# Matmuls of zeros between the first maximum passes and between the last scores of a cross-attention and expert kernel

## The chip, the core and the metric

The kernel runs on one core of a Trainium2 chip. A core has TensorE (matmuls, writing to PSUM, PE in the profile), VectorE (DVE), ScalarE (ACT), GpSimd (POOL) and DMA queues that SyncE (SP) and others fill. The metric is the device time of one execution in microseconds; the lower the better. A time is given as the median of several runs, and one further execution was recorded by the hardware profiler.

## What is computed

Eight samples x of 256 channels by 512 positions get a cross attention with 16 heads of 16 channels each (queries from the layer-normed x, keys and values from a context), and then a mixture of eight experts, two per row, with a shared expert. Cut to the attention:

```python
q = einsum('oc,bct->bot', Wq, layernorm(x)) + bq      # k and v from ctx, with Wk, Wv
q = q.reshape(B, H, K, T)                             # H = 16 heads, K = 16, T = 512
scores = einsum('bhkt,bhks->bhts', q, k) * SCALE
p = softmax(scores, axis=-1)
out = einsum('bhts,bhks->bhkt', p, v).reshape(B, H * K, T)
x = x + einsum('oc,bct->bot', Wo, out) + bo
x = x + ffn(layernorm(x))    # rmsnorm, router, top 2 of 8 experts, and a shared expert
```

## The kernel before

The attention is cut into 16 halves (`HALVES`): a half is eight heads of one sample. Each half has 32 units (`UNITS`): a unit is one head and one quarter (128) of the 512 positions.

For a softmax without overflow the kernel first needs the maximum of each row of scores. So it computes scores twice. A **maximum pass** (`max_pass`, line 560, tile `smax_ps`, three banks) multiplies queries by keys with the queries' positions on the partitions; VectorE reduces each bank to a column of `negmax` (line 665, semaphore `max_done`). When a half's 32 units are done, `turn_max` (line 574) transposes the maxima, VectorE splits them into two parts (lines 672 and 674), and the SP queue carries them to DRAM and back into two extra rows of the query stack (lines 337 and 345, semaphore `rows_loaded`). The **scores** proper (`scores`, line 586, tile `st_ps`, three banks) then come out with the maximum subtracted, and ScalarE takes their exponential into `probs` (line 490, `exp_done`). After each group of four units a step `pv` (line 599, tile `pv_ps`) multiplies the probabilities by the values; after four such steps ScalarE copies the sums out (line 481), and they travel over DRAM to be divided. Maximum passes and scores use only 48 or 50 of the array's 128 rows, and two of them, of different row halves, run side by side.

The tensor engine's order is written out by hand. First four opening matmuls of zeros (line 510), then the projections of the halves 0 and 1 (`project_qk`, line 533, and `project_v`, line 544). Then the prologue: all 32 maximum passes of half 0, with the projections of half 2 in between; `turn_max(0)`; and the first 24 (`LEAD`) passes of half 1. Then the main loop over slots s = 0 to 15: for each pair of units two scores of half s, two maximum passes 24 units ahead, and at fixed u a `pv` step, a projection of half s + 3, the turn of the maxima, or (in odd slots, `OUT_UNITS`) a step of the output projection (`project_out`, line 232). In slot 14 the passes end at u = 6; from u = 8 there, and in all of slot 15, no maximum passes are left, and no projections but four steps of the output projection late in slot 15.

A score for unit i waits for the exponential of unit i - 3, since there are three banks; a maximum pass for unit i waits for the reduction of unit i - 3. VectorE, between the maxima of half 0 and those of half 1, computes row statistics of the last samples (line 246). Behind the main loop comes the stage of the shared expert and routing, and then 39 expert blocks (lines 1045 to 1086). `zeros` is a tile of 128 by 512 zeros in fp32 that VectorE sets at the start.

Of the kernel before, what the change touches and what calls it, by code (L numbers as in the profile page):

```python
# [13 lines left out]
P = 128  # L14
# [3 lines left out]
HALVES = 2 * B  # L18
# [3 lines left out]
GH = 4  # L22
UNITS = HH * TT
STEPS = UNITS // GH
LEAD = 24
# [4 lines left out]
TILES = 2  # L30
# [16 lines left out]
def xattn_ffn_kernel(nc, x, ctxt, wqkv_t, wo_t, bias_cols, rms_w, router_t, gate_up, down,  # L47
# [18 lines left out]
    with ExitStack() as outer:  # L66
        def sem(name):
            return outer.enter_context(nc.semaphore(name))

        def sb(name, shape, dt=F32, stack=outer):  # L70
            return stack.enter_context(nc.sbuf_tensor(name, shape, dt))
# [3 lines left out]
        zeros = sb("zeros", [P, D])  # L75
# [28 lines left out]
        def aps(name, shape, dt=F32):  # L104
            return attn_ctx.enter_context(nc.psum_tensor(name, shape, dt))
# [16 lines left out]
        pv_ps = aps("pv_ps", [P, T])  # L122
# [23 lines left out]
        max_done = sem("max_done")  # L146
# [38 lines left out]
        def out_batch(s):  # L185

            return (s - 3) // 2 if s % 2 == 1 and s >= 3 else None

        def smax_bank(i):
            return smax_ps[:, i % MAXBUF, :]  # L190
# [34 lines left out]
        def project_out(pe, b, o, kt, bank):  # L225
            if kt == 0 and o == 0:
                pe.wait_ge(attn_ready, ATTN_START + 2 * (b + 1))
                pe.wait_ge(vt_copied, min(2 * b + 7, HALVES))
                pe.wait_ge(nm_parts_ready, min(2 * b + 5, HALVES))
            if kt == 0 and (b > 0 or o > 0):  # L230
                pe.wait_ge(x1_ready, X1_START + 2 * b + o)
            mm = nc.tensor.matmul(bank, w_o[:, kt, o * P:(o + 1) * P], attn[:, b % 2, kt, :],  # L232
                                  start=(kt == 0), stop=(kt == CT - 1))
            if kt == CT - 1:
                mm.then_inc(y_ready, 1)
# [63 lines left out]
        with nc.Block() as block:  # L299
# [207 lines left out]
            def _(pe):  # L507
# [5 lines left out]
                for o in range(CT):  # L513
                    for kt in range(CT):
                        mm = nc.tensor.matmul(pv_ps[:, o:o + 1], w_o[:, kt, o * P:(o + 1) * P], bv_col[:, kt:kt + 1],
                                              start=(kt == 0), stop=(kt == CT - 1))
                mm.then_inc(bo_ready, 1)

                def project_qk(n, i, kt):
                    if kt == 0 and i == 0:  # L520
                        pe.wait_ge(c_loaded[(n // 2) % 2], 16 * (n // 4 + 1))
                        if n >= FIRST:
                            pe.wait_ge(vt_copied, n)
                            pe.wait_ge(nm_parts_ready, n - 2)
                        if out_batch(n - 4) is not None:
                            pe.wait_ge(x1_ready, X1_START + CT * (out_batch(n - 4) + 1))
                        if 1 <= n < 3:
                            pe.wait_ge(vt_copied, n)
                    elif kt == 0:
                        pe.wait_ge(qk32_ready, 2 * n + 1)  # L530
                        pe.wait_ge(xn_ready, n // 2 + 1)
                    src = c_sb[:, (n // 2) % 2, :, :] if i == 0 else xn
                    mm = nc.tensor.matmul(proj_ps[:, :], w_t[:, i, kt, (n % 2) * P:(n % 2) * P + P],  # L533
                                          src[:, kt, :], start=(kt == 0), stop=(kt == CT - 1))
                    if kt == CT - 1:
                        mm.then_inc(qk_ready, 1)

                def project_v(n, st):
                    if st == 0:
                        pe.wait_ge(qk32_ready, 2 * n + 2)  # L540
                        if n >= FIRST:
                            pe.wait_ge(nm_parts_ready, n - 1)
                    for kt in range(CT):
                        mm = nc.tensor.matmul(proj_ps[:, st * P:(st + 1) * P],  # L544
                                              c_sb[:, (n // 2) % 2, kt, st * P:(st + 1) * P],
                                              w_t[:, 2, kt, (n % 2) * P:(n % 2) * P + P],
                                              start=(kt == 0), stop=(kt == CT - 1))
                    if st == TT - 1:
                        mm.then_inc(v_ready, 1)

                def max_pass(n, u):
                    buf = n % NBUF
                    if u == 0:
                        pe.wait_ge(stack_loaded[buf], 16 * 2 * 2 * TILES * (n // NBUF + 1))
                    i = UNITS * n + u
                    if i >= MAXBUF:
                        pe.wait_ge(max_done, i - MAXBUF + 1)
                    tile, pair, tt = u % TILES, u // TILES // TT, u // TILES % TT
                    low = HALFP * tile
                    nc.tensor.matmul(smax_bank(i), q_stack[buf][low:low + SROWS, pair, tt * P:(tt + 1) * P],  # L560
                                     k_stack[buf][low:low + SROWS, pair, :], start=True, stop=True,
                                     tile_position=(low, 0)).then_inc(s_ready, 1)

                def turn_max(n):
                    if n == 0:
                        pe.wait_ge(vt_copied, FIRST)
                    else:
                        pe.wait_ge(qk32_ready, 2 * min(n + 3, HALVES))
                        pe.wait_ge(vt_copied, min(n + 2, HALVES))
                        pe.wait_ge(nm_parts_ready, n)  # L570
                    if n > 0 and out_batch(n - 2) is not None:
                        pe.wait_ge(x1_ready, X1_START + CT * (out_batch(n - 2) + 1))
                    pe.wait_ge(max_done, UNITS * (n + 1))
                    nc.tensor.transpose(proj_ps[0:UNITS, 0:P], negmax[:, n % 2, :], ident[:, :]).then_inc(nm_turned, 1)

                def scores(s, u):
                    g, st, j = u // (GH * TT), u // GH % TT, u % GH
                    buf = s % NBUF
                    if u == 0:
                        pe.wait_ge(rows_loaded[buf], 16 * TILES * (s // NBUF + 1))  # L580
                        pe.wait_ge(ones_loaded, 16 * TILES * NBUF)
                    i = UNITS * s + u
                    if i >= STBUF:
                        pe.wait_ge(exp_done, i - STBUF + 1)
                    low, pair, end = HALFP * (j % TILES), 2 * g + j // TILES, HALFP * (j % TILES) + SROWS + PARTS
                    nc.tensor.matmul(score_bank(i), k_stack[buf][low:end, pair, st * P:(st + 1) * P],  # L586
                                     q_stack[buf][low:end, pair, :], start=True, stop=True,
                                     tile_position=(low, 0)).then_inc(st_ready, 1)
# [16 lines left out]
                for n in range(2):  # L605
# [3 lines left out]
                    for st in range(TT):  # L609
                        project_v(n, st)  # L610
                pe.wait_ge(ident_ready, 2)
                for u in range(UNITS):
                    max_pass(0, u)
                    if u in (0, 2, 8, 10):
                        project_qk(2, u // 8, u % 8 // 2)
                    if 16 <= u < 16 + TT:
                        project_v(2, u - 16)
                turn_max(0)
                for u in range(LEAD):
                    max_pass(1, u)  # L620

                for s in range(HALVES):
                    proj = s + 3 < HALVES
                    for u in range(0, UNITS, TILES):
                        scores(s, u)
                        scores(s, u + 1)
                        n = s + 1 + (u + LEAD) // UNITS
                        if n < HALVES:
                            max_pass(n, (u + LEAD) % UNITS)
                            max_pass(n, (u + LEAD) % UNITS + 1)  # L630
                        if u % GH == 0 and STEPS * s + u // GH >= 1:
                            pv(STEPS * s + u // GH - 1)
                        if proj and u in (0, 2, 6, 8):
                            project_qk(s + 3, u // 6, u % 6 // 2)
                        if proj and 14 <= u < 14 + 2 * TT:
                            project_v(s + 3, (u - 14) // 2)
                        if u == 12 and s + 1 < HALVES:
                            turn_max(s + 1)
                        if out_batch(s) is not None and u in OUT_UNITS:
                            project_out(pe, out_batch(s), OUT_UNITS.index(u) // CT, OUT_UNITS.index(u) % CT, proj_ps[:, :])  # L640
                pv(STEPS * HALVES - 1)
# [650 lines left out]
```

## Time and profile before

| | before |
|---|---|
| median of 3 runs | 988.53 us (981.55 to 991.89) |
| the profiled execution | 987.59 us |
| its span, first to last instruction | 985.7 us |
| mean granted TensorE clock | 0.903 |
| TensorE busy | 885.4 us, 90% |
| VectorE busy | 463.3 us, 47% |
| ScalarE busy | 408.1 us, 41% |

A row of the profile's timeline gives the start in us from the span's start, the duration in us, the engine, the line of the kernel, the operation, and its output and input tiles by name; behind it the idle time before it and who ended that. Several instructions of one kind in a row are merged, x2 and so on; each then lasts a little beyond the start of the next row, since matmuls are pipelined. A matmul of fp32 operands stands as two instructions; a score or a maximum pass (fp32r) as one. PE is TensorE's matmul, PEld its weight load. The granted clock is given as a share of full speed (2.4 GHz).

### The profile page before, as it was taken

Reading aid. Unit: us, or ns where it says so; the run is one execution under the profiler, and the core shown is the slowest. Engines: PE = TensorE matmul, PEld = TensorE weight load, DVE = VectorE, ACT = ScalarE, POOL = GpSimd, SP = SyncE. Lnnn points to the kernel's source line nnn. Section 1 sums busy time; section 2 is a strip of 40 time slices with the busy share of each in tenths; the row PEclk is TensorE's granted clock in tenths of the full one; section 3 lists DMA queues with packets and bytes.
Section 4 is the critical chain, followed back from the end, with each engine's and each line's share of the span. In section 5 each row is a group of like instructions: output and inputs, shape, how many; then the busy total and the mean of one; then the engine's idle time right before and its main releaser. Section 6 shows DMA issues by size and latency. Waiting matters only on the chain. (4 is left out here: it accounts for less than half of the span.)

```text
span 985.7 us, 10816 instructions
## 1 busy us (share of the span) xinstructions
PE 885.4 (90%) x3616; PEld 376.5 (38%) x3616; DVE 463.3 (47%) x894; ACT 408.1 (41%) x753; POOL 253.6 (26%) x239
## 2 busy tenths in 40 slices
PE   7679999898998989999998998899399999999992
PEld 3233333333333333333332225654144444444441
DVE  3577777676776765777786006451121111111110
ACT  1103676655666565666667542320002222222320
POOL 3100221413214131231110000317312444444431
PEclk8755999999999997999997557989699999999997
DMA  6772455546645565255521104941132455545552
GB/s 218 191 174 94 114 135 132 132 90 151 143 101 128 94 153 127 64 130 132 130 51 27 24 22 155 393 171 44 45 111 60 86 89 96 93 87 88 92 88 32
DMA packets 47877, 110.56 MB, mean 112 GB/s; under 512 B 12704, under 2 KB 13728, under 8 KB 43520
## 3 DMA queue, kind: packets, MB, share of 16 engines
q1 hardware_dynamic: 35376, 80.26, 31.7%
q0 software_dynamic: 12416, 29.48, 14.6%
q8 instruction: 31, 0.51, 0.2%
q14 instruction: 22, 0.18, 0.1%
q10 hardware_dynamic: 32, 0.13, 0.0%
HBM read 68.48 MB, written 41.23 MB: 111 GB/s over the span
## 5 line engine op out<-in xcount | busy, mean ns | idle before, releaser
L665 DVE TENSOR_REDUCE negmax<-smax_ps 128x1 f32<-128x512 f32 x512 | 325.5, 683 | 131.1 <-PE smax_ps L560 130.0
L490 ACT ACTIVATE probs<-st_ps 128x512 f32<-128x512 f32 x512 | 273.7, 603 | 155.1 <-PE st_ps L586 154.9
L586 PE MATMUL st_ps<-q_stack,k_stack 50*128 50x512 f32 x512 | 163.9, 522 | 20.5 <-ACT probs L490 20.5
L560 PE MATMUL smax_ps<-k_stack,q_stack 48*128 48x512 f32 x512 | 144.0, 456 | 13.9 <-DVE negmax L665 7.3
L599 PE MATMUL pv_ps<-probs,v_t 128*32 128x512 f32 x1024 | 148.9, 656 | 3.6 <-ACT probs L490 1.7
L1086 PE MATMUL big_ps<-w_gu,attn 128*128 x312 | 140.4, 593 | 0.8 <-ACT attn L934 0.8
L586 PEld LDWEIGHTS st_ps<-q_stack,k_stack 50*128 50x128 f32 x512 | 63.0, 197 | 178.0 <-ACT probs L490 116.4
L898 POOL DMA_INDIRECT out<-x_sb,row_i x39 | 61.1, 1568 | 147.6 <-ACT x_sb L941 140.7
L560 PEld LDWEIGHTS smax_ps<-k_stack,q_stack 48*128 48x128 f32 x512 | 67.7, 200 | 38.4 <-DVE negmax L665 26.0
L1239 DVE TENSOR_TENSOR zeros<-attn,big_ps 128x256 f32<-128x256 f32 x39 | 16.4, 421 | 135.0 <-ACT attn L953 135.0
L1086 PEld LDWEIGHTS big_ps<-w_gu,attn 128*128 128x128 f32 x312 | 56.2, 190 | 57.0 <-issue 57.0
L287 POOL TENSOR_TENSOR attn<-attn,recip 128x512 f32<-128x512 f32 x15 | 19.1, 1275 | 227.1 <-DMA recip<-rec_dram 227.1
L1054 PE MATMUL big_ps<-rows_or_down,zeros 128*128 x156 | 73.5, 593 | 0.6 <-DVE zeros L1231 0.6
L401 POOL CAST parts<-qk 128x512 fp32r<-128x512 f32 x26 | 15.8, 609 | 193.3 <-ACT qk L449 193.3
L987 PE MATMUL big_ps<-ht_all,sh_gu 128*128 128x512 f32 x128 | 62.2, 645 | 1.8 <-DVE pv_raw L1113 1.8
L953 ACT ACTIVATE attn<-big_ps 128x256 f32<-128x256 f32 x39 | 14.9, 383 | 117.7 <-PE big_ps L1086 117.7
L405 POOL TENSOR_TENSOR parts<-qk,parts 128x512 fp32r<-128x512 f32 x32 | 40.9, 1279 | 41.2 <-DVE parts L658 39.1
L533 PE MATMUL proj_ps<-c_sb,w_t 128*128 128x512 f32 x64 | 42.4, 755 | 8.2 <-DMA c_sb<-in_ctx 7.1
L544 PEld LDWEIGHTS proj_ps<-w_t,c_sb 128*128 128x128 f32 x256 | 34.5, 198 | 38.9 <-issue 35.6
L544 PE MATMUL proj_ps<-w_t,c_sb 128*128 128x128 f32 x256 | 45.6, 307 | 3.5 <-ACT qk L449 1.6
L941 ACT ACTIVATE x_sb<-big_ps,meta_blocks 128x512 f32<-128x512 f32 x39 | 26.8, 687 | 45.0 <-PE big_ps L1054 25.9
L881 POOL DMA_INDIRECT x_sb<-h_rows,row_i x39 | 38.6, 990 | 23.6 <-DMA out<-x_sb 12.0
(135 smaller groups left out, 687.0 us busy)
## 6 DMA issues: line engine op xcount, KB each, us to landing
parts_dram<-parts SPq DMA_DIRECT2D x32, 512.0 KB, 4.6
k_stack<-parts_dram SPq DMA_DIRECT2D x32, 256.0 KB, 4.6
q_stack<-parts_dram SPq DMA_DIRECT2D x32, 256.0 KB, 5.2
w_gu<-in_gate_up SPq DMA_DIRECT2D x8, 1024.0 KB, 13.0
x_sb<-in_x SPq DMA_DIRECT2D x8, 512.0 KB, 7.2
c_sb<-in_ctx POOLq DMA_DIRECT2D x8, 512.0 KB, 5.1
k_stack<-parts_dram SPq DMA_DIRECT2D x32, 128.0 KB, 4.7
q_stack<-parts_dram SPq DMA_DIRECT2D x32, 128.0 KB, 5.6
```

The source lines that it names most:

```text
L405: nc.gpsimd.tensor_tensor(parts[:, i, 1, :], qk32[:, i, :], parts[:, i, 0, :].bitcast(F32), ALU.subtract).then_inc(low_ready, 1)
L490: nc.scalar.activation(probs[:, k % 2, u % GH, :], score_bank(UNITS * s + u), ACT.Exp, scale=SCALE).then_inc(exp_done, 1)
L533: mm = nc.tensor.matmul(proj_ps[:, :], w_t[:, i, kt, (n % 2) * P:(n % 2) * P + P], src[:, kt, :], start=(kt == 0), stop=(kt == CT - 1))
L544: mm = nc.tensor.matmul(proj_ps[:, st * P:(st + 1) * P], c_sb[:, (n // 2) % 2, kt, st * P:(st + 1) * P], w_t[:, 2, kt, (n % 2) * P:(n % 2) ...
L560: nc.tensor.matmul(smax_bank(i), q_stack[buf][low:low + SROWS, pair, tt * P:(tt + 1) * P], k_stack[buf][low:low + SROWS, pair, :], start=T ...
L586: nc.tensor.matmul(score_bank(i), k_stack[buf][low:end, pair, st * P:(st + 1) * P], q_stack[buf][low:end, pair, :], start=True, stop=True, ...
L599: mm = nc.tensor.matmul(pv_ps[32 * j:32 * j + 32, :], v_t[n % NBUF][:, st, GH * g + j, :], probs[:, k % 2, j, :], start=(st == 0), stop=(s ...
L665: nc.vector.tensor_reduce(negmax[:, n % 2, c:c + 1], smax_bank(UNITS * n + u), AX_X, ALU.max, negate=True).then_inc(max_done, 1)
L898: nc.gpsimd.indirect_dma_start(out_rows, bass.IndirectOffsetOnAxis(ap=row_i[:, k:k + 1], axis=0), y_sb[:, k % RING, :], None, compute_op=A ...
L987: mm = nc.tensor.matmul(big_ps[:, 2 * (j % 2) + i, :], sh_gu[:, a, i * F + c * P:i * F + (c + 1) * P], ht_all[:, g, a, :], start=(a == 0), ...
L1054: mm = nc.tensor.matmul(y_ps[:, k % 2, :], act_t[:, a, :], w_dn[:, bass.ds(expert, 1), a, :], start=(a == 0), stop=(a == FT - 1))
L1086: mm = nc.tensor.matmul(gu_ps[:, :], h_t[:, k % 2, a, :], w_gu[:, bass.ds(expert, 1), a, :], start=(a == 0), stop=(a == DT - 1))
```

## The change

A function `filler` is added: one matmul of zeros by zeros, 128x128 by 128x512 in fp32, whose result nobody reads. It is issued at three places: after every second maximum pass of half 0 (16 times) and of the first 24 passes of half 1 (12 times), into the bank `pv_ps`, which nothing else uses then; and in the last two slots, from u = 10 of slot 14 on at every fourth u (2, 6, 10, ...), after the second score of the pair, 14 times, into the first bank of `smax_ps`. The first of these waits until all 512 maxima are taken. Nothing is removed, and no other engine gets other work.

```diff
--- before.py
+++ after.py
@@ -609,8 +609,14 @@
                     for st in range(TT):
                         project_v(n, st)
                 pe.wait_ge(ident_ready, 2)
+
+                def filler(bank):
+                    nc.tensor.matmul(bank, zeros[:, 0:P], zeros[:, :], start=True, stop=True)
+
                 for u in range(UNITS):
                     max_pass(0, u)
+                    if u % TILES == 1:
+                        filler(pv_ps[:, :])
                     if u in (0, 2, 8, 10):
                         project_qk(2, u // 8, u % 8 // 2)
                     if 16 <= u < 16 + TT:
@@ -618,6 +624,8 @@
                 turn_max(0)
                 for u in range(LEAD):
                     max_pass(1, u)
+                    if u % TILES == 1:
+                        filler(pv_ps[:, :])
 
                 for s in range(HALVES):
                     proj = s + 3 < HALVES
@@ -636,6 +644,10 @@
                             project_v(s + 3, (u - 14) // 2)
                         if u == 12 and s + 1 < HALVES:
                             turn_max(s + 1)
+                        if UNITS * s + u + LEAD >= UNITS * (HALVES - 1) and u % GH == 2:
+                            if UNITS * s + u + LEAD < UNITS * (HALVES - 1) + GH:
+                                pe.wait_ge(max_done, UNITS * HALVES)
+                            filler(smax_bank(0))
                         if out_batch(s) is not None and u in OUT_UNITS:
                             project_out(pe, out_batch(s), OUT_UNITS.index(u) // CT, OUT_UNITS.index(u) % CT, proj_ps[:, :])
                 pv(STEPS * HALVES - 1)
```

TensorE's order at the start of the prologue, before the change: the first maximum passes of half 0 (`smax_ps`) with projections of half 2 between them.

```order
L560 MATMUL smax_ps<-k_stack,q_stack 128x512 [waits stack_loaded0,ident_ready]
L533 MATMUL proj_ps<-c_sb,w_t 128x512 [waits vt_copied,c_loaded1]
L560 MATMUL smax_ps<-k_stack,q_stack 128x512 x2
L533 MATMUL proj_ps<-c_sb,w_t 128x512
L560 MATMUL smax_ps<-k_stack,q_stack 128x512 [waits max_done] x6
L533 MATMUL proj_ps<-xn,w_t 128x512 [waits xn_ready,qk32_ready]
L560 MATMUL smax_ps<-k_stack,q_stack 128x512 [waits max_done] x2
```

The same place with the change: a matmul of zeros (line 614) stands behind each second pass.

```order
L560 MATMUL smax_ps<-k_stack,q_stack 128x512 [waits stack_loaded0,ident_ready]
L533 MATMUL proj_ps<-c_sb,w_t 128x512 [waits vt_copied,c_loaded1]
L560 MATMUL smax_ps<-k_stack,q_stack 128x512
L614 MATMUL pv_ps<-zeros 128x512
L560 MATMUL smax_ps<-k_stack,q_stack 128x512
L533 MATMUL proj_ps<-c_sb,w_t 128x512
L560 MATMUL smax_ps<-k_stack,q_stack 128x512 [waits max_done]
L614 MATMUL pv_ps<-zeros 128x512
L560 MATMUL smax_ps<-k_stack,q_stack 128x512 [waits max_done] x2
L614 MATMUL pv_ps<-zeros 128x512
L560 MATMUL smax_ps<-k_stack,q_stack 128x512 [waits max_done] x2
```

Every pair of passes now has a filler behind it; the projections keep their places.

TensorE's order in slot 14 from the scores u = 10 on, before the change, with the turn of the last maxima (`ident,negmax`):

```order
L586 MATMUL st_ps<-q_stack,k_stack 128x512 [waits exp_done] x4
L599 MATMUL pv_ps<-probs,v_t 32x512 [waits exp_done]
L599 MATMUL pv_ps<-probs,v_t 32x512 x3
L574 MATMUL proj_ps<-ident,negmax 32x128 [waits x1_ready,nm_parts_ready,max_done,vt_copied,qk32_ready]
L586 MATMUL st_ps<-q_stack,k_stack 128x512 [waits exp_done] x4
L599 MATMUL pv_ps<-probs,v_t 32x512 [waits exp_done]
L599 MATMUL pv_ps<-probs,v_t 32x512 x3
L586 MATMUL st_ps<-q_stack,k_stack 128x512 [waits exp_done] x4
```

The same place with the change:

```order
L586 MATMUL st_ps<-q_stack,k_stack 128x512 [waits exp_done] x2
L614 MATMUL smax_ps<-zeros 128x512 [waits max_done]
L586 MATMUL st_ps<-q_stack,k_stack 128x512 [waits exp_done] x2
L599 MATMUL pv_ps<-probs,v_t 32x512 [waits exp_done]
L599 MATMUL pv_ps<-probs,v_t 32x512 x3
L574 MATMUL proj_ps<-ident,negmax 32x128 [waits x1_ready,nm_parts_ready,max_done,vt_copied,qk32_ready]
L586 MATMUL st_ps<-q_stack,k_stack 128x512 [waits exp_done] x2
L614 MATMUL smax_ps<-zeros 128x512
L586 MATMUL st_ps<-q_stack,k_stack 128x512 [waits exp_done] x2
L599 MATMUL pv_ps<-probs,v_t 32x512 [waits exp_done]
L599 MATMUL pv_ps<-probs,v_t 32x512 x3
```

The four scores between two `pv` steps are split two and two by a filler, and the first filler brings the wait for `max_done` ahead of one pair of scores and one `pv` step.

## Rows read from the trace of the kernel before

**Rows 1.** the page, part 2: granted TensorE clock in 40 slices, in tenths
```profile
PEclk8755999999999997999997557989699999999997
```

**Rows 2.** windows: stretch, length, busy us PE, PEld, DVE, ACT, POOL, clock, DMA
```profile
80.00:85.00 5.00, 5.00 (x10) 2.42 (x9) 5.00 (x10) 0.00 (x0) 0.00 (x0) 0.50 0.16 66
550.00:555.00 5.00, 4.74 (x20) 0.98 (x12) 0.00 (x0) 2.33 (x5) 0.00 (x0) 0.50 0.00 0
```

**Rows 3.** timeline of TensorE, prologue: start us, us, instruction, [idle before]
```profile
39.76 1.54 PE L533 MATMUL proj_ps<-c_sb,w_t 128*128 128x512 f32 x2
41.23 0.74 PE L560 MATMUL smax_ps<-k_stack,q_stack 48*128 48x512 f32 x3
...
44.16 2.08 PE L533 MATMUL proj_ps<-xn,w_t 128*128 128x512 f32 x2
```

**Rows 4.** timeline of TensorE, turn of maxima to main loop
```profile
67.41 0.37 PE L574 MATMUL proj_ps<-ident,negmax 128*32 128x128 f32 x1 [1.09 <-DVE negmax L665]
...
74.69 12.74 PE L560 MATMUL smax_ps<-k_stack,q_stack 48*128 48x512 f32 x21 [5.76 <-DVE negmax L665]
86.75 1.11 PE L586 MATMUL st_ps<-q_stack,k_stack 50*128 50x512 f32 x2
...
94.87 1.23 PE L599 MATMUL pv_ps<-probs,v_t 128*32 128x512 f32 x8
```

**Rows 5.** timeline of VectorE, row statistics and then maxima of the second half
```profile
68.33 4.83 DVE L246 BATCH_NORM_STATS2 stats<-x_sb 128x6 f32<-128x512 f32 x8
...
73.95 15.63 DVE L665 TENSOR_REDUCE negmax<-smax_ps 128x1 f32<-128x512 f32 x26
```

**Rows 6.** timeline of TensorE, main loop at full clock
```profile
514.56 0.40 PE L560 MATMUL smax_ps<-k_stack,q_stack 48*128 48x512 f32 x2
514.89 1.06 PE L599 MATMUL pv_ps<-probs,v_t 128*32 128x512 f32 x8
515.88 1.12 PE L232 MATMUL proj_ps<-attn,w_o 128*128 128x512 f32 x2
516.94 0.50 PE L586 MATMUL st_ps<-q_stack,k_stack 50*128 50x512 f32 x2
```

**Rows 7.** timeline of TensorE, last two slots
```profile
538.96 1.22 PE L586 MATMUL st_ps<-q_stack,k_stack 50*128 50x512 f32 x3
...
549.55 1.93 PE L599 MATMUL pv_ps<-probs,v_t 128*32 128x512 f32 x8
551.41 1.22 PE L586 MATMUL st_ps<-q_stack,k_stack 50*128 50x512 f32 x3
552.89 0.79 PE L586 MATMUL st_ps<-q_stack,k_stack 50*128 50x512 f32 x1 [0.26 <-ACT probs L490]
553.62 1.94 PE L599 MATMUL pv_ps<-probs,v_t 128*32 128x512 f32 x8
...
580.39 0.79 PE L586 MATMUL st_ps<-q_stack,k_stack 50*128 50x512 f32 x2
...
585.70 1.64 PE L232 MATMUL proj_ps<-attn,w_o 128*128 128x512 f32 x2
587.27 0.50 PE L586 MATMUL st_ps<-q_stack,k_stack 50*128 50x512 f32 x2
...
593.41 1.06 PE L599 MATMUL pv_ps<-probs,v_t 128*32 128x512 f32 x8 [1.18 <-ACT probs L490]
```

**Rows 8.** timeline of ScalarE: first table load, then last two slots
```profile
87.59 1.28 ACT L490 ACT_TABLE_LOAD   x1 [27.72 <-PE st_ps L586]
...
560.87 0.59 ACT L481 ACTIVATE pv_raw<-pv_ps 128x512 f32<-128x512 f32 x1
...
587.81 1.08 ACT L490 ACTIVATE probs<-st_ps 128x512 f32<-128x512 f32 x2 [2.78 <-PE st_ps L586]
```

**Rows 9.** timeline of TensorE, the opening matmuls of zeros
```profile
1.52 6.16 PE L510 MATMUL pv_ps<-zeros 128*128 128x512 f32 x8 [1.52 <-DVE zeros L677]
```

**Rows 10.** timeline of the SP queue, load of the turned maxima
```profile
541.23 0.56 SPq L345 DMA_DIRECT2D q_stack<-rows_dram  x2
```

## Prediction

> **What bounds the kernel now.** I read the page's clock row first [rows 1]: in forty slices, each of 24.6 us, TensorE's granted clock is at about half in the third and fourth (49 to 99 us) and again from the 22nd to the 24th (517 to 591 us). The windows then say what it did there [rows 2]: at 80 to 85 us it counts as busy all the time at 0.50, and at 550 to 555 us it is busy 4.74 of 5 us, again at 0.50. The two levels, 1.00 and 0.50, are 2.4 and 1.2 GHz. Between the two stretches the main loop runs at full clock.
>
> First stretch. While only maximum passes run, VectorE sets the pace: 26 maxima take 15.63 us, 0.60 us each [rows 5]; TensorE waits for free banks, and that wait is hidden in its "busy". Once the main loop begins, at 86.75, the half clock costs: from there to the first probs x V product it needs 8.12 us, and the clock rises within that product, at about 95.3 (it lasts 1.23 us, between the 1.06 and the 1.93 of others) [rows 4, 6, 7].
>
> Second stretch, the last two slots. No maximum passes are left, a group of four scores and one probs x V step repeats, and the rows show its period: product start to product start 4.07 us, of which the product takes 1.86, three scores and a short wait for ScalarE 1.48, the last score 0.73 [rows 7]. Ten such groups lie between 538.96 and 580.39, so 41.43 us. TensorE at half clock is most of this chain, ScalarE idles. At 586.8 the clock rises: two output projections stood among the scores before it, and the projection at 585.70 takes 1.57 us up to the next score, instead of 2.0.
>
> **Price of a filler.** It has the shape of a projection step (128x128 by 128x512 in fp32, two instructions). At full clock such a step advances TensorE by 1.06 us (515.88 to 516.94) [rows 6]; at half it lasts 2.08 with its tail, about 2.00 without [rows 3]. The lower bound is the opening run of four matmuls of zeros, 8 instructions in 6.16 us, 1.54 per matmul [rows 9]: if none of it was at full clock, a filler at full clock costs half of that, 0.8. I take 1.06 and 2.00, since each filler stands between other shapes, as the projections do. A pair of scores or maxima costs 0.34 at full clock [rows 6] and about 0.72 at half [rows 7].
>
> **Prologue, first 32 passes (16 fillers).** The present rows show what projections mixed with passes do: after one projection step and two passes TensorE was in a second step when the clock went up, at about 40.7 (the step at 39.76 advances it 1.47, not 2.0); passes alone followed, and at 44.16 a projection is back at 2.08 [rows 3]. The first filler stands where such a mixture stands now, so I expect the same rise at 40.7, and then no fall, since TensorE has no gap. At full clock: 16 fillers x 1.06 = 17.0, 4 projection steps 4.2, 4 value projections about 2.6, 10 pairs 3.4, 12 single passes about 3.6: 30.8; plus 2.2 for the half-clock start (first pass a little over 3 us ahead of 39.76, at 36.3): to 69.3, and 1.1 for the last maximum to come out: 70.4, against the turn at 67.41 [rows 4]. VectorE (32 x 0.60 = 19.2) is no longer the limit. **+3.0 us.**
>
> **Prologue, the next 24 passes (12 fillers).** Three passes and one filler go at once, then TensorE waits while VectorE does row statistics: 68.33 to 73.95, some 6.5 us from turn to first maximum [rows 5, 4]. The clock will fall there. Afterwards, from u = 3 on, TensorE needs 11 fillers and about 10.5 pairs: 15.4 us at full clock, against 12.06 now (74.69 to 86.75), because a pair with its filler costs 1.40 where two maxima cost 1.20. The pace at half is 2.72. For how long it stays half is not shown; the mixture is that ahead of 40.7, which did rise, and the similar one of 86.75 to 95.3 needed 8.5 us. Taking 7 us at half adds 3.5: 18.9, **+6.8 us**. Then the main loop begins at full clock: in place of 8.12 us ScalarE's chain (table load, four exponentials) allows about 4.5 (1.28, four times 0.50 and two latencies of 0.54) [rows 8], and the product is 0.1 shorter: **-3.7 us**. Prologue in all: **+6.1 us**.
>
> **Last two slots (14 fillers).** The first filler waits for all maxima; but the transpose one pair of scores later waits for the same count anyway. That filler runs while ScalarE loads tables, which hides all but 0.45 us. At full clock the period has two candidates. The chain: score to exponential 0.54 (587.27 to 587.81), two exponentials 1.08 [rows 8], signal 0.08, product 1.00 [rows 6]: 2.70. TensorE's own work: two pairs 0.68, filler 1.06, product 1.00: 2.74. So the filler just fits into the hole; I take 2.75. Three of the ten groups have ScalarE's copy of the sums in their chain, 0.59 with 0.1 overlapped [rows 8]: 3.2. Ten groups: 7 x 2.75 + 3 x 3.2 = 28.9 instead of 41.4, **-12.6 us**. Against it: the 0.45, and the time at half before the rise. At half a group costs 0.72 + 2.00 + 0.72 + 1.87 = 5.3. I assume 3.6 us of it past 539, which loses 3.6 x (1 - 2.75 / 5.3) = 1.7. The final five pairs of scores with four projection steps, three products and now three fillers sum to 1.7 + 4.2 + 3.0 + 3.2 = 12.1, with the last exponentials some 12.5, where 580.39 to 594.4 was 14.0 [rows 7]: **-1.5 us**. In all **-12.0 us**. Next late could be the rows of the turned maxima: their load into the query stack goes out at 541.23 [rows 10], and by my pace the scores that need it come at about 552 (4.5 groups after 539.4), so the load has some 10 us.
>
> What follows (row statistics, shared experts, expert blocks) only shifts.
>
> **Sum.** +6.1 - 12.0 = -5.9 us. The profiled span is 985.7 and its run 987.6, so 981.7 for that run; the median 988.5 lies 0.9 above, so 982.5.
>
> **A rule against it.** At 550 to 555 us TensorE idles 0.26 us of 5 and is still at 1.2 GHz, as it is through the whole stretch [rows 2]. The Trainium skill (TensorE: Matmul & The Clock Gate, section "HAM oscillation — how this bites in real kernels") blames idle gaps between bursts for the lower clock. By that rule a stretch with such short gaps should have risen unaided, and fillers, which close gaps that hardly exist, would buy no clock. The rows do not agree with the rule on the first point, and that is why I let the rises at 40.7, 95.3 and 586.8, each behind projections, carry the forecast.
>
> **Rivals.**
> - The clock stays at half behind the fillers in the last slots. For it: TensorE is busy 95% there (4.74 of 5 us) without a rise. Against it: projections inserted into the same pattern raised it at 586.8 and at 95.3, and the opening zeros end sooner than eight instructions of 1.0 would [rows 9]. Price: ten groups at 5.3 instead of 4.14, +12, and three fillers at the end, +4; with the prologue's +6 that is +22: about 1010. It decides from the point where more than half of the stretch is at half clock (5.3 h + 2.75 (1 - h) = 4.14 gives h = 0.55). Chance 0.07. It is the case that the rule gives.
> - The same in the second part of the prologue only: 11.5 pairs x 2.72 = 31.3 instead of 12.06, +19, and no -3.7; with +3.0 and -12.0 the sum is +10: 998. Chance 0.08.
> - The fillers cost less and the clock is regained at once: 0.8 instead of 1.06 for 26 prologue fillers is -7 where VectorE does not catch it (it does from 1.20 per pair, so -5), no time at half in the second part gives -3.5, the end -1.7 more: -16, so 972. A half-way case is 977. Speaks for it: the rise at 40.7 came after only two steps. Against it: the wait for row statistics. Chance 0.27.
> - My forecast, 979 to 990 with the phase of the clock: 0.58.
>
> **Numbers.** A run pair of this kernel can tell about 1% (10 us) from no change. Faster by over 1% (below 978.6): 0.27; within: 0.58; slower: 0.15. Eight in ten: from the good rival's 973 to 995, which leaves out the two bad ones' upper ends.
>
> **What would show it.** Right: clock at 1.0 from about 41 to 71 us, the turn of the first maxima at about 70, the first score at about 95, then full clock; in the last slots product-to-product 2.75 us soon after 540, and the shared stage starting some 6 us earlier. Wrong: a clock row still at half at 550 us with a period of 5.3, or pairs at 2.72 up to the first score; or, the other way, pairs at 1.20 in the prologue.

## The result, and the profile after

| | before | changed |
|---|---|---|
| median | 990.22 us (979.22 to 996.18, 20 runs) | 997.89 us (987.84 to 1010.7, 20 runs) |
| ratio, 95% interval | | 1.0079 (1.005 to 1.0107) |
| the profiled execution | 987.59 us | 987.84 us |
| its span | 985.7 us | 986.1 us |
| mean granted clock | 0.903 | 0.940 |

The change costs 0.8%, some 8 us. The profiled execution of the changed kernel is the quickest of its twenty, 10 us below their median. So it shows where time went in a lucky case, and what the others have on top must come from further profiles. A ratio leaves out executions over 1.5% above their kernel's fastest, while the medians shown are over all, so the two can differ.

The page's clock row of the changed kernel, to be held against [rows 1]: the long half-clock stretches in the third and fourth slice and in the 22nd to 24th are mostly gone, and a new one stands in the fifth.

```profile
PEclk7997699999999999999999797989699999999997
```

TensorE in the prologue, timeline of the changed kernel (start, duration, instruction, idle before):

```profile
35.67 0.47 PE L560 MATMUL smax_ps<-k_stack,q_stack 48*128 48x512 f32 x1 [2.81 <-DMA q_stack<-parts_dram]
...
37.12 0.49 PE L560 MATMUL smax_ps<-k_stack,q_stack 48*128 48x512 f32 x1
37.54 1.12 PE L614 MATMUL pv_ps<-zeros 128*128 128x512 f32 x2
38.60 0.49 PE L560 MATMUL smax_ps<-k_stack,q_stack 48*128 48x512 f32 x1
...
41.55 0.49 PE L560 MATMUL smax_ps<-k_stack,q_stack 48*128 48x512 f32 x2
41.98 1.13 PE L614 MATMUL pv_ps<-zeros 128*128 128x512 f32 x2
43.03 0.49 PE L560 MATMUL smax_ps<-k_stack,q_stack 48*128 48x512 f32 x2
...
68.73 0.27 PE L574 MATMUL proj_ps<-ident,negmax 128*32 128x128 f32 x1 [0.41 <-DVE negmax L677]
...
75.91 0.79 PE L560 MATMUL smax_ps<-k_stack,q_stack 48*128 48x512 f32 x1 [4.99 <-DVE negmax L677]
76.63 2.07 PE L614 MATMUL pv_ps<-zeros 128*128 128x512 f32 x2
78.64 0.79 PE L560 MATMUL smax_ps<-k_stack,q_stack 48*128 48x512 f32 x2
```

Where [rows 3] had half-speed projections, each filler here advances TensorE by 1.06 us (37.54 to 38.60), a pair of passes with its filler by 1.48 (41.55 to 43.03), and the first pass already finds full clock; TensorE had idled 2.81 us before it. The turn of the first maxima is at 68.73, against 67.41 in [rows 4]. During the row statistics (4.99 us idle at 75.91) the clock falls, and a filler costs 2.01 us (76.63 to 78.64).

The main loop's start, the same timeline of TensorE, and then ScalarE's at that place (the table loads):

```profile
101.67 1.06 PE L599 MATMUL pv_ps<-probs,v_t 128*32 128x512 f32 x8
...
106.26 0.72 PE L586 MATMUL st_ps<-q_stack,k_stack 50*128 50x512 f32 x1 [1.37 <-ACT probs L490]
...
107.33 1.94 PE L599 MATMUL pv_ps<-probs,v_t 128*32 128x512 f32 x8
```

```profile
102.79 1.28 ACT L297 ACT_TABLE_LOAD   x1
104.08 0.21 ACT L297 ACTIVATE rs_b<-rs_a 128x8 f32<-128x8 f32 x1
104.31 1.28 ACT L490 ACT_TABLE_LOAD   x1
```

The first probs x V product is at 101.67 (before at 94.87, [rows 4]). The table loads for the square root of the last samples, in slot 0, keep TensorE idle for 1.37 us; by the next product, at 107.33, it lasts 1.94, so the clock is at half again.

The last two slots, the same timeline, to be held against [rows 7]:

```profile
550.17 2.07 PE L614 MATMUL smax_ps<-zeros 128*128 128x512 f32 x2
...
552.90 1.34 PE L599 MATMUL pv_ps<-probs,v_t 128*32 128x512 f32 x8
...
562.35 1.06 PE L599 MATMUL pv_ps<-probs,v_t 128*32 128x512 f32 x8
563.35 0.49 PE L586 MATMUL st_ps<-q_stack,k_stack 50*128 50x512 f32 x2
563.77 1.12 PE L614 MATMUL smax_ps<-zeros 128*128 128x512 f32 x2
564.83 0.49 PE L586 MATMUL st_ps<-q_stack,k_stack 50*128 50x512 f32 x2
565.25 1.06 PE L599 MATMUL pv_ps<-probs,v_t 128*32 128x512 f32 x8
...
595.47 1.07 PE L599 MATMUL pv_ps<-probs,v_t 128*32 128x512 f32 x8
```

The first filler meets half clock (2.07 us with its tail); within the product at 552.90 the clock rises. From then on the period is 2.90 us (562.35 to 565.25), where it was 4.07. The last product is at 595.47.

Stage by stage, from the same landmarks in each profile (us between them; "turn" is the transpose of a half's maxima, "product" a `pv` step):

| stretch | before | changed | changed once more (e10) |
|---|---|---|---|
| first pass to first turn | 31.1 | 33.1 | 40.1 |
| first turn to first product | 27.5 | 32.9 | 35.6 |
| first product to second turn | 10.0 | 14.1 | 14.2 |
| second turn to last turn | 433.8 | 438.4 | 434.6 |
| last turn to last product | 54.8 | 41.3 | 41.3 |

The two profiles of one kernel differ by 7.0 us in the first stretch and by 2.7 in the second, so a difference of a few us between two profiles says little.

### The profile page after: what moved, and what is told of

The parts are those of the page before. It is cut to its first block and busy times, and to the rows that moved or that the text cites. A ratio compares the mean times of both kernels' runs of the same rounds, so it can differ in the third digit from the quotient of the medians.

```text
span 986.1 us, 10984 instructions
## 1 busy us (share of the span) xinstructions
PE 897.7 (91%) x3700; PEld 377.8 (38%) x3700; DVE 465.4 (47%) x894; ACT 409.0 (41%) x753; POOL 254.0 (26%) x239
## 5 line engine op out<-in xcount | busy, mean ns | idle before, releaser
L586 PE MATMUL st_ps<-q_stack,k_stack 50*128 50x512 f32 x512 | 153.7, 503 | 16.3 <-ACT probs L490 16.3
L599 PE MATMUL pv_ps<-probs,v_t 128*32 128x512 f32 x1024 | 141.0, 623 | 2.4 <-ACT probs L490 0.9
L560 PE MATMUL smax_ps<-k_stack,q_stack 48*128 48x512 f32 x512 | 132.6, 435 | 8.2 <-DVE negmax L677 5.3
L586 PEld LDWEIGHTS st_ps<-q_stack,k_stack 50*128 50x128 f32 x512 | 59.0, 188 | 167.3 <-ACT probs L490 117.9
L560 PEld LDWEIGHTS smax_ps<-k_stack,q_stack 48*128 48x128 f32 x512 | 61.4, 193 | 37.9 <-DVE negmax L677 28.6
L893 POOL DMA_INDIRECT x_sb<-h_rows,row_i x39 | 38.7, 992 | 24.5 <-DMA out<-x_sb 12.9
```

The costliest lines, as they stand in the source:

```text
L599: mm = nc.tensor.matmul(pv_ps[32 * j:32 * j + 32, :], v_t[n % NBUF][:, st, GH * g + j, :], probs[:, k % 2, j, :], start=(st == 0), stop=(s ...
```

## Experiments

Each kernel is the changed one with the edit shown, or the one before with the part named. "Ratio" is always to the kernel before on the same chip. The kernels ran on several chips, where before itself had medians of 992.6, 998.5, 974.7 and 995.3 us; so ratios are compared, not times. The profiles differ by chip behind the last product: from there to the end took 373 to 380 us in the three on the chip where before has 974.7, and 391 to 399 in the other thirteen.

**e1: the last slots' fillers alone.**

```diff
                 for u in range(UNITS):
                     max_pass(0, u)
-                    if u % TILES == 1:
-                        filler(pv_ps[:, :])
                 for u in range(LEAD):
                     max_pass(1, u)
-                    if u % TILES == 1:
-                        filler(pv_ps[:, :])
```

> Only the 14 fillers of the last two slots; the prologue is that of before. Theory A (the prologue's fillers lose more than they seem to, the last slots gain as forecast): from the turn of the last maxima to the last product some 41 us instead of 54.8, and in all 11 to 14 us faster than before, about 977. Theory B (the gain in the last slots was luck of the one profiled execution, and in most executions the clock stays at half behind those fillers): less than 5 us faster, and times scattered by more than 15 us.

Measured: ratio 0.9886 (0.9822 to 0.995); last turn at 542.53 and last product at 584.67, so 42.1 us. Theory A, at the low end of its 11 to 14 us: the median of all six runs lies 9.5 us below that of before. Repeated later on another chip (e13):

> The kernel with the 14 fillers of the last slots alone, again, on the chip of the neighbours. If its gain belongs to the kernel: 0.985 to 0.992. If the 1.1% was drawn by chance or by the chip: nearer 0.995.

Measured: 0.9847 (0.9777 to 0.9917), 41.3 us for the stretch (546.67 to 588.00). A gain of over 1% on both chips is the kernel's own.

**e2: the prologue's fillers alone** (the block with `smax_bank(0)` taken out).

> Only the 28 fillers of the prologue; the last slots are those of before. Theory A: 18 to 24 us slower than before, the whole of the last slots' gain and the net loss together, about 1010. Theory B: 6 to 10 us slower, what the forecast gave for the prologue with a little on top, about 998.

Measured: ratio 1.0194 (1.0142 to 1.0247), 1010.9 us. Theory A: the prologue loses 1.9%, some 19 us, where the forecast had 6. With e1's -1.1% that makes +0.8%, the whole result.

**e3 and e4: the prologue's two halves apart** (e3 keeps the filler behind `max_pass(0, u)`, e4 the one behind `max_pass(1, u)`).

> Only the 16 fillers among the first 32 maximum passes. Theory A: about 3 us slower, as forecast, since the clock falls again in the row statistics and the rest runs as before. If the prologue's loss sits here, over 8 us slower.

> Only the 12 fillers among the 24 passes of half 1. Theory A: most of the loss sits here, 12 to 20 us slower than before: the passes take 20 us instead of 12, and TensorE, at full clock by the main loop's start, runs into ScalarE's table loads of slot 0, is idle over 1 us there and falls to half clock for some 15 us. Theory B: 4 to 6 us slower, the fillers' own time, with no fall.

Measured: e3 1.0085 (1.0039 to 1.0131), e4 1.0109 (1.007 to 1.0148). Their sum is e2's 1.94%. Neither theory had this split: e3 costs 8 us where 3 were forecast. How the loss divides between the two is less sure than the ratios make it seem: by the medians of all runs on that chip e3 is 10.9 us above before and e4 4.2. TensorE's timeline in e3 shows why:

```profile
36.25 0.76 PE L560 MATMUL smax_ps<-k_stack,q_stack 48*128 48x512 f32 x1 [4.63 <-DMA q_stack<-parts_dram]
36.94 2.07 PE L533 MATMUL proj_ps<-c_sb,w_t 128*128 128x512 f32 x2
...
39.67 2.07 PE L614 MATMUL pv_ps<-zeros 128*128 128x512 f32 x2
41.67 0.79 PE L560 MATMUL smax_ps<-k_stack,q_stack 48*128 48x512 f32 x1
...
66.94 1.78 PE L614 MATMUL pv_ps<-zeros 128*128 128x512 f32 x2
68.65 0.50 PE L560 MATMUL smax_ps<-k_stack,q_stack 48*128 48x512 f32 x1
...
84.04 0.27 PE L574 MATMUL proj_ps<-ident,negmax 128*32 128x128 f32 x1 [0.41 <-DVE negmax L671]
```

The same mixture as in the changed kernel, but the first pass found half clock (0.76 us instead of 0.47), and it stayed: fillers of 2.00 us up to the one at 66.94, some 31 us long, and the turn of the first maxima at 84.04. TensorE is not short of work there: from 37 to 67 us the windows show it busy all the time, at 0.50. In e4, which has no fillers there, the turn is at 67.65, and in e1 at 67.53. In e4 the first turn to the first product takes 31.0 us (67.65 to 98.63), 3.5 more than before.

**e10: the changed kernel once more.**

> The changed kernel once more, one look. Its median lies 10 us above its first profiled execution. If the time TensorE spends at half clock among the first 32 passes differs from execution to execution (0, 17, 17 and 34 us in the four kernels with these fillers profiled so far), the turn of the first maxima comes here at 72 to 86 us, not at 68.7. If the fillers usually find the clock up, at 68 to 70.

Measured: one run of 976.85 us on a chip where before has 974.72. TensorE's timeline:

```profile
36.25 0.76 PE L560 MATMUL smax_ps<-k_stack,q_stack 48*128 48x512 f32 x1 [4.60 <-DMA q_stack<-parts_dram]
...
76.39 0.27 PE L574 MATMUL proj_ps<-ident,negmax 128*32 128x128 f32 x1 [0.41 <-DVE negmax L677]
...
112.02 1.07 PE L599 MATMUL pv_ps<-probs,v_t 128*32 128x512 f32 x8
...
116.60 0.79 PE L586 MATMUL st_ps<-q_stack,k_stack 50*128 50x512 f32 x1 [1.36 <-ACT probs L490]
...
117.75 1.93 PE L599 MATMUL pv_ps<-probs,v_t 128*32 128x512 f32 x8
```

The first pass at half clock, the turn at 76.39: 40.1 us instead of 33.1, with the clock at half for 17 us by the windows. The second fall is here too, behind the same wait (1.36 us at 116.60). In all the kernels with the first 16 fillers this far (the changed one, e2, e3, e5, e10) the time at half clock between 30 and 70 us was 0, 17, 34, 17 and 17 us, and the turn came at 68.7, 75.9, 84.0, 76.5 and 76.4. The lucky case is the one whose profile was taken first.

Set beside the ten profiles that have no filler in this stretch, these show what the clock costs with and without them (us, from the first pass to the first turn):

| profiles | fillers | of it at half clock | length |
|---|---|---|---|
| e6, e11, e13, e14 | none | 23 | 30.1 to 30.2 |
| before, e7, e9 | none | 28 | 31.1 to 31.2 |
| e1, e4, e12 | none | 32 | 32.1 to 32.2 |
| changed | 16 | 0 | 33.1 |
| e2, e5, e10 | 16 | 14 to 15 | 39.3 to 40.1 |
| e3 | 16 | 32 | 47.8 |

Without fillers, nine us more at half clock cost 2.1 us; with them, 14 to 15 us at half cost 6.2 to 7.0, twice as much per us.

**e8: two fillers behind each second pass, among the first 32 passes alone.**

```diff
                     if u % TILES == 1:
                         filler(pv_ps[:, :])
+                        filler(pv_ps[:, :])
```

> Only the first 32 passes, but two fillers behind each second pass instead of one (32 fillers). Theory M, the mixture of one filler and a pair of passes is at the margin at which the clock rises: with two it rises within 10 us of 36, and the turn of the first maxima comes at 86 to 92, though 16 more fillers stand there; the one-filler kernel had it at 84.0 and 75.9 with 34 and 17 us at half. Theory N, zeros don't lift the clock in this place whatever their share: all at half, turn at 115 or later.

Measured: ratio 1.0299 (1.0229 to 1.037), from two runs. TensorE's timeline:

```profile
37.52 0.76 PE L560 MATMUL smax_ps<-k_stack,q_stack 48*128 48x512 f32 x1 [6.60 <-DMA q_stack<-parts_dram]
...
40.94 3.60 PE L614 MATMUL pv_ps<-zeros 128*128 128x512 f32 x4
44.47 0.50 PE L560 MATMUL smax_ps<-k_stack,q_stack 48*128 48x512 f32 x1
44.90 1.12 PE L533 MATMUL proj_ps<-c_sb,w_t 128*128 128x512 f32 x2
...
87.00 0.27 PE L574 MATMUL proj_ps<-ident,negmax 128*32 128x128 f32 x1
```

The first two fillers take 3.53 us together, more at half clock than not, and from 44.47 on everything is at full clock. The turn is at 87.00: with twice the fillers hardly later than e3's 84.04. Theory M, as far as one profile tells; theory N, all at half, is out. With one filler per pair of passes the clock rose later in four of five profiles, in e3 after 34 us.

**e5: the changed kernel, with the square root ahead of the first score.**

```diff
                 act.wait_ge(ones_loaded, 16 * TILES * NBUF)
+                std(act, 4 * CT, B * CT, 2)
...
-                        if s == 0 and u == 5:
-                            std(act, 4 * CT, B * CT, 2)
```

> The changed kernel with all its fillers, and ScalarE's square root for the last samples (with its two table loads) taken out of slot 0, u = 5, and put ahead of the first score, where ScalarE idles. If the second fall of the clock at 106 us and the 3 to 4 us between the first product and the turn of slot 0 come from these table loads, the first product to the next turn takes about 10 us instead of 14.1, and the kernel is 3 to 6 us faster than the changed one (990 to 995). If it is only chance there, no difference that can be told.

Measured: ratio 0.9918 (0.9857 to 0.9978), against 1.0079 for the changed kernel. TensorE's timeline, first product, third product and the turn of slot 0:

```profile
106.15 1.07 PE L598 MATMUL pv_ps<-probs,v_t 128*32 128x512 f32 x8
...
113.59 1.06 PE L598 MATMUL pv_ps<-probs,v_t 128*32 128x512 f32 x8
114.58 0.28 PE L573 MATMUL proj_ps<-ident,negmax 128*32 128x128 f32 x1
```

First product to second turn 8.4 us, where the changed kernel had 14.1 and 14.2, and the products stay at 1.06. The 5.7 us are the wait for the table loads and the fall behind it together, and not all of them are due to the fillers: without fillers among the 24 passes this stretch took 10.0 to 12.9 us in eight profiles, and 8.4 to 8.6 with the same move (e6, e9, e12). The ratio moved by more than 5.7 us (1.6%, 16 us), but the medians of e5 and of before on that chip, 999.8 and 998.5, show no gain. What the move brings in the total stays open.

**e6: the same move with the last slots' fillers alone.**

> The same move with the fillers of the last two slots alone. The waits of TensorE for the table loads in slot 0 (about 1 to 2 us) go, so 1 to 3 us faster than the last slots' fillers alone: ratio 0.985 to 0.988. If the clock falls more often without the early work, no gain: 0.989.

Measured: 0.9813 (0.9749 to 0.9878); first product to second turn 8.4 us again (91.18 to 99.61), where e1 has 11.1. The interval overlaps those of e1 and e13.

**e7: two more fillers in slot 14**, into the bank `proj_ps`, which is free there once the residuals are taken.

```diff
+                        if s == HALVES - 2 and u in (2, 6):
+                            pe.wait_ge(x1_ready, X1_START + CT * (out_batch(HALVES - 3) + 1))
+                            filler(proj_ps[:, :])
```

> The last slots' fillers plus two more in slot 14, at u = 2 and 6, where TensorE waits for ScalarE's table loads and the clock falls. If a filler there keeps the clock up, the 8 to 14 us at half clock around 530 to 545 go and the kernel gains 2 to 4 us on the last slots' fillers alone. If the wait is too long for one filler, the clock falls all the same and the two cost 0 to 2 us.

Measured: 0.9861 (0.982 to 0.9903), no difference to e1 that can be told. TensorE's timeline:

```profile
528.68 1.13 PE L614 MATMUL proj_ps<-zeros 128*128 128x512 f32 x2
...
533.48 0.49 PE L586 MATMUL st_ps<-q_stack,k_stack 50*128 50x512 f32 x1 [1.10 <-ACT probs L490]
...
534.14 1.27 PE L614 MATMUL proj_ps<-zeros 128*128 128x512 f32 x2
535.35 0.79 PE L586 MATMUL st_ps<-q_stack,k_stack 50*128 50x512 f32 x2
...
538.56 1.12 PE L614 MATMUL smax_ps<-zeros 128*128 128x512 f32 x2
```

The filler at 528.68 does not bridge ScalarE's table loads (1.10 us idle at 533.48); the clock falls during the next one and is back by 538.56, so 3.4 us at half, where e1 had 13.7. Yet the turn of slot 13 to that of slot 14 takes 32.7 us in e7 and 32.8 in e1. So the clock was mostly kept and bought nothing. Either ScalarE's table loads set the pace there and cover TensorE's clock, or the two fillers, 1.05 and 1.21 us, took what the clock gave; no run tells these apart.

**e11: fillers in slot 14 only**, none in slot 15.

> Of the fillers only the six in slot 14, none in slot 15. If scores and products alone hold the full clock once it is up, slot 15's groups take 2.7 us without a filler in place of 2.9, and the kernel is 1 to 3 us faster than with all 14 (ratio 0.985 to 0.988). If the clock falls without them, slot 15 runs at 4.1 us per group again and half or more of the gain is gone (0.993 to 0.997).

Measured: 0.9938 (0.9893 to 0.9983) on the chip where before has 974.7. The ratio lies in the second range (the clock falls), but the medians of all runs give 0.9886, and the profile shows the first case. TensorE's timeline in slot 15, and windows (stretch, length, busy us of PE, PEld, DVE, ACT and POOL, granted clock, DMA):

```profile
562.77 1.06 PE L599 MATMUL pv_ps<-probs,v_t 128*32 128x512 f32 x8 [0.48 <-ACT probs L490]
563.76 0.73 PE L586 MATMUL st_ps<-q_stack,k_stack 50*128 50x512 f32 x3
564.95 0.49 PE L586 MATMUL st_ps<-q_stack,k_stack 50*128 50x512 f32 x1 [0.45 <-ACT probs L490]
565.44 1.07 PE L599 MATMUL pv_ps<-probs,v_t 128*32 128x512 f32 x8
```

```profile
560.00:565.00 5.00, 3.63 (x24) 1.06 (x16) 0.00 (x0) 4.06 (x9) 0.00 (x0) 1.00 0.19 31
570.00:575.00 5.00, 3.78 (x23) 1.05 (x23) 0.00 (x0) 4.25 (x9) 0.50 (x1) 1.00 0.18 53
```

Full clock holds with no filler, at a busy time of 3.6 and 3.8 of 5 us. The period is 2.67 us, the chain that the prediction had at 2.70; last turn to last product takes 39.8 us instead of 41.3. So in this profile scores and products hold the clock without fillers, and slot 15's cost 1.5 us. e12, below, has none there either, and its clock fell once, 3.4 us by the windows, inside the product at 571.59; it rose again within a step of the output projection:

```profile
571.59 1.85 PE L598 MATMUL pv_ps<-probs,v_t 128*32 128x512 f32 x8 [0.48 <-ACT probs L491]
...
574.10 1.63 PE L232 MATMUL proj_ps<-attn,w_o 128*128 128x512 f32 x2
```

In the eight profiles with slot 15's fillers there is no fall in that slot. So the clock can hold without fillers, but it is not certain to.

**e9 and e12: combined.** e9 is e7 with e5's move; e12 is e9 without slot 15's fillers.

> No fillers in the prologue; those of the last two slots, the two more in slot 14, and the square root of the last samples ahead of the first score. If the three gains add, 1.9 to 2.3% faster than before (ratio 0.977 to 0.981), with 8.4 us from the first product to the next turn and under 5 us at half clock around slot 14. If the two small ones are chance, 0.986 to 0.989 as with the last slots' fillers alone.

> Fillers in slot 14 only (the six of the change and two at u = 2 and 6), the square root of the last samples ahead of the first score, nothing in the prologue and in slot 15. If the parts add: 1 to 3 us faster than the combined kernel with slot 15's fillers, and the best of all; against before on its own chip 0.978 to 0.990, and 2 to 6 us below the last slots' fillers alone on the same chip.

Measured: e9 0.9917 (0.988 to 0.9954) on the chip of e11; e12 0.985 (0.9778 to 0.9922) on that of e13, where e13 has 0.9847. The landmarks are near the plan (e12: 8.4 us from first product to second turn, 41.0 from last turn to last product; e9: 8.6 and 41.3, with 6.8 us at half clock around slot 14 where under 5 were expected), but the total shows no gain over the last slots' fillers alone. e9 missed both its ranges; e12's ratio is inside its own, but it is not the best of all and not 2 to 6 us below e13 (medians 982.2 and 981.7). What covers the few us saved is in part plain: the long stretch from second to last turn took 429 to 456 us in the sixteen profiled executions, whatever the edit, because the clock falls there here and there for 3 to 14 us: 12 us in all at half clock in e3, where the stretch is shortest (429.4), and 56 in e8, where it is longest (456.1). Effects of 2 or 3 us don't stand out from that.

**e14: before once more.**

> The kernel before, one look on the same chip. From the turn of the last maxima to the last product 54 to 55 us as before if the half clock in the last slots is no chance of the first profile; 42 to 50 if the clock sometimes rises there by itself.

Measured: 54.7 us (556.22 to 610.94); the half clock in the last slots is no chance. All six profiles without fillers there (before, e2, e3, e4, e8, e14) stay at half for 55 to 58 us. This execution took 1004.6 us, and 450.4 of them lie between the second and the last turn, 16.6 more than in the first profile, with 48 us at half clock instead of 24.

The version to keep is e1's: before with the 14 fillers of the last two slots, 1.1 and 1.5% faster than before in its two measurements; e6 and e12 cannot be told from it.

## Why the prediction was wrong

The forecast was 982.5 us, and within 1% the likeliest; measured is 0.8% slower, 997.9 us, outside the range up to 995. The step that failed is the prologue, forecast at +6.1 us and measured at some 19 (e2). Two things in it were wrong: the **first 32 passes**, where the clock was to rise at 40.7 "and then no fall", and the **main loop that "begins at full clock"** behind the next 24, where the wait for the square root's table loads in slot 0, and a fall of the clock behind it, had no term.

- **Last two slots, forecast -12.0 us: right.** e1 alone gives -1.1% (11 us) and -1.5%; the stretch from last turn to last product shrank by 13.5 us. Some of this can be given back later: from the last product to the end e1, e6 and e13 took 397.5 to 398.5 us, while the six profiles without these fillers took 391.8 to 393.4 (the four others with them, on the same chips, 390.6 to 395.5). The period came to 2.90, not 2.75: with a filler between them each of the two pairs of scores costs 0.42 (563.35 to 563.77, 564.83 to 565.25), not the 0.34 taken from a pair ahead of another pair. The chain without the filler, 2.70, was right to 0.03 (e11).
- **Price of a filler, 1.06 and 2.00: right** (1.06 and 2.01 measured).
- **First 32 passes, forecast +3.0: wrong, +8 measured (e3), +10.9 by the medians.** The prediction took one rise in one profile for a property of the mixture. That rise is not even certain for the old mixture: in ten profiles without fillers there the clock rose at 39 to 41 us in six, at 47 in one (e7), and not before 80 in three (e1, e4, e12). At full clock all the way the stretch took 33.1 us against 31.1, +2.0. But in four of the five executions seen with these 16 fillers the clock was at half for 17 or 34 us, and on average over the five the stretch took 40.1 us against 31.1 in the ten without, +9.0. That one filler per pair is too few and two are enough is what e8 suggests; it is one profile, so that part is not shown.
- **What makes it a loss.** Two maxima take VectorE 1.20 us, and TensorE needs about 0.7 for the two passes at half clock, so without fillers half clock costs little there (the table under e10). A filler turns 1.20 into 1.48 at full clock (forecast 1.40: the passes beside a filler cost 0.42, not 0.34) and into 2.72 at half. It makes a stage that hardly felt the clock pay for it: at 32 us of half clock, 47.8 us with fillers and 32.1 without.
- **Next 24 passes, forecast +6.8, then -3.7: too low, and the end wrong.** First turn to first product took 32.0 us on average in the five profiles with these fillers and 27.0 in the eleven without, +5.0 (forecast +3.1). 7 us at half clock behind the row statistics were assumed; it was about 5 in e2, e4 and e5, 10 in the changed kernel and 16 in e10. What was missing is the next late thing: with TensorE at full clock at the loop's start, the table loads of slot 0 left it idle for 1.4 us, and in both profiles of the changed kernel the clock then fell for 17 us; first product to second turn took 14.1 and 14.2 us. In e2 and e4, with the same fillers in this stage, the fall was 3.4 us and the stretch 11.8 and 11.9, no more than the 10.0 to 12.9 without fillers. So this too is a draw. With the move of the table loads there is no fall there (e5, e6, e12).
- **What stays open.** The three stretches together give +15.6 us on average (9.0, 5.0 and 1.6), and e2 measures 18 to 19; the other 3 us I cannot place.
- **The rivals.** The second rival, half clock through the second part of the prologue, had the sum of 998, and 997.9 was measured; that is luck. Its +19 us did not come in that part, where the clock rose in every profile before the first score; the loss is spread over three stretches, the largest of them the first. Its own price is also uneven: it counts 11.5 pairs at 2.72 where the forecast has 11 fillers and 10.5 pairs, and the third rival counts 26 fillers of the prologue's 28; neither moves a time by over 2 us. The rival of the page's rule, half clock in the last slots, did not come: there the fillers raised the clock in every kernel that has them. The Trainium skill (TensorE: Matmul & The Clock Gate, section "HAM oscillation — how this bites in real kernels") ties the lower clock to idle gaps. In the prologue of e3 TensorE has hardly a gap and stays at 1.2 GHz, while slot 15 of e11 idles over 1 us of 5 at 2.4 GHz; so gaps alone don't decide, in either direction. The fall in the wait of 4.99 us for the row statistics agrees with the section; the one behind the table loads came after only 1.37 us of idle time, far less than the waits that the section describes.

## What to carry to other kernels

Before filling TensorE to raise its clock, ask which engine sets the pace of that stage: where another engine does, half clock is nearly free, and every filler is a cost that half clock doubles (1.06 and 2.01 us here). Fillers pay where TensorE at half clock is itself in the chain and a hole in the chain at full clock is about as long as the filler (slot 15: 2.67 us per group without, 2.90 with). A rise seen once in one profile is one draw; look at the same place in several executions before a term of the sum rests on it.

## What the runs showed of the hardware

- The clock has a memory: in slot 15 scores and products alone hold 2.4 GHz in e11 (busy 3.6 and 3.8 of 5 us in the windows shown), and the same work does not leave 1.2 GHz in before (busy 4.74 of 5 us, [rows 2]) from 539 to 580 us.
- Matmuls of zeros count towards the rise: in the last slots the six profiles without fillers stay at half clock for 55 to 58 us, and the nine that meet half clock there with fillers for 3 to 14.
- Among the first passes two fillers in a row had the clock up 7 us after the first pass (e8); with one it took 14 to 15 us in three profiles and 32 in a fourth.
- The idle time ahead of the first pass was 2.81 us in the changed kernel's first profile, where the clock had not fallen, and 4.5 to 7.1 us in the other fifteen, where it had.
- One program takes different courses from execution to execution: the changed kernel spent 0 us at half clock among its first 32 passes in one profile and 15 in the other, and its runs span 988 to 1011 us.
